# Second expert layer, mixing of a token's two expert outputs: the first scaling on ScalarE, the scaled addition on VectorE

## The chip, the cores and the metric

One core of a Trainium2 chip runs the kernel. The metric is the device time in microseconds, the median over runs. A profiled execution gives the rows below; it is one execution, and its own time is given beside its span.

The engines are named as in the profile: PE is TensorE's matmul, PEld its weight load, DVE is VectorE, ACT is ScalarE, POOL is GpSimd and SP is SyncE.

## What is computed

The model has four blocks, each an attention and an expert layer, on 2 x 1024 tokens of width 256. The change lies in the expert layer of the second block. For each token it takes the two experts with the largest gate, mixes their outputs with the gates as weights and multiplies the mixture by one more matrix:

```python
gating = jax.nn.softmax(X @ Wg + bg, axis=-1)
top_k_indices = jnp.argsort(gating, axis=-1)[..., -TOPK:]      # TOPK = 2, 8 experts
h1 = jnp.einsum('bsd,edh->bseh', X, W1) + b1
h3 = jnp.einsum('bsd,edh->bseh', X, W3) + b3
h = jax.nn.silu(h1 * h3)
expert_outputs = jnp.einsum('bseh,eho->bseo', h, W2) + b2
topk_out = jnp.take_along_axis(expert_outputs, top_k_indices[..., None], axis=2)
topk_w = jnp.take_along_axis(gating, top_k_indices, axis=-1)
mixed = jnp.sum(topk_w[..., None] * topk_out, axis=2)
return mixed @ Wf + bf
...
x = x + jnp.tanh(g_ffn[1]) * _L1_ffn_ref(_layernorm(x, axis=-1), ...)
```

The last four lines of the function, from `topk_out` on, and the addition to `x` are the part that the change is about.

## The kernel before

The layer is `l1_ffn`. It keeps 2048 tokens as 16 tiles of 128 (`TILES`), 256 columns each. Every engine has a program of its own, written out in order, and engines wait for each other on semaphores; no scheduler moves anything. Between two layers all engines meet at a barrier, so the next layer (an attention) starts when the last engine has ended this one.

Most of the layer is a loop over experts and their tiles of routed tokens. It ends with each token's two expert outputs in the memory `outs`. Then comes the mixing, which is all that the change touches:

- SyncE loads the first outputs, ScalarE the second ones, in four quarters of four tiles each (`load_outputs`, L896), into `fetched[:, k, t, :]`. The quarter's two loads count up `fetched_part[q]`. All eight loads are issued at once, after `all_stored`.
- VectorE makes the mixture of tile t in `mixed[:, t % 4, :]`, a ring of four buffers. L1157 multiplies the first output by its weight (a tensor_scalar with a pointer operand), L1158 multiplies the second by its own and adds L1157's result (a scalar_tensor_tensor). Both go through `Steps`: it counts `mix_steps` up when the instruction is complete and makes VectorE itself wait for that count before it goes on. Behind the mixture of tile t VectorE adds tile t - 2 to `x` (`add_output`, L1148).
- TensorE transposes the mixture in two pieces (`turn_mixed`, L1017) into one of two banks of `p_h`. It then multiplies by `wf` (L1029, two matmuls of 256 columns, each of which stands as two rows in the profile) into one of two other banks. Its order is: transposition of tile t + 1, then product of tile t. The product of tile t waits for `added`, the addition of tile t - 2.
- ScalarE copies the transposed mixture from the bank to `mixed_t` (L1066), a ring of four.

In the prediction "transposition of tile t", "copy of tile t", "product of tile t" and "addition of tile t" are these steps.

## Time and profile before

| | us |
|---|---|
| median of three runs | 3202.24 |
| lowest and highest | 3200.54, 3202.68 |
| profiled execution, its own time | 3204.76 |
| its span | 3203.0 |
| TensorE busy | 2851.1 (89%) |
| VectorE busy | 1890.4 (59%) |
| ScalarE busy | 1432.0 (45%) |
| GpSimd busy | 586.9 (18%) |
| TensorE's granted clock, mean | 0.931 |

The busy times are averages over some ten layers with different limits. The mixing runs from the first landing at 1010.76 us to the end of the last addition at 1035.78 us. What happens in it is read from the windows, the waits and the timeline of that stretch. The timeline joins rows of one kind; "x4" is four rows, and "x8" at the end are the products of two tiles. The bracket at the end of a row is the idle time of the engine before it, and what ended it. A row of the windows gives the stretch, its length, then the busy time (and the count of instructions) of PE, PEld, DVE, ACT and POOL, the granted clock, the busy share of the DMA engines and what they moved. The granted clock is given as a share: 1.00 is 2.4 GHz and 0.50 is 1.2 GHz.

### The profile page before, as it was taken

How to read it: one execution, taken by the hardware profiler on the slowest of the kernel's cores; microseconds unless marked ns; L12 is line 12 of the kernel's file. 1: busy time of each engine (PE TensorE's matmuls, PEld its weight loads, DVE VectorE, ACT ScalarE, POOL GpSimd, SP SyncE). 2: the span in 40 equal slices, each digit the busy share in tenths (PEclk: the TensorE clock that was granted, in tenths of full speed). 3: DMA queues.
4: the chain of work that ended last, by engine and by line, in shares of the span. 5: the costliest groups of instructions: out<-in, count | busy, mean ns of one | idle time of the engine just before them, and what ended most of it. 6: DMA issues, size and time to landing. Idle time of an engine off the chain costs nothing. (4 is left out here: it accounts for less than half of the span.)

```text
span 3203.0 us, 46363 instructions
## 1 busy us (share of the span) xinstructions
PE 2851.1 (89%) x13988; PEld 2126.9 (66%) x13989; DVE 1890.4 (59%) x3602; ACT 1432.0 (45%) x2987; POOL 586.9 (18%) x655
## 2 busy tenths in 40 slices
PE   5796779986997989999689999999999999968996
PEld 4795545546886779999456666666666666646665
DVE  4414465516555354443588888878788888664443
ACT  1233544431211224544347766767676777711111
POOL 0133010001442200000200000000000000106776
PEclk8698879996999779999799999999999999979999
DMA  1342022223232010000112323233222332335776
GB/s 40 107 163 92 1 32 23 22 11 117 84 103 81 13 40 27 26 13 1 24 25 24 31 22 31 22 33 31 31 21 30 23 31 22 13 72 149 162 173 144
DMA packets 153723, 168.84 MB, mean 53 GB/s; under 512 B 38128, under 2 KB 123014, under 8 KB 153286
## 3 DMA queue, kind: packets, MB, share of 16 engines
q1 hardware_dynamic: 115878, 105.16, 20.2%
q0 software_dynamic: 21280, 37.93, 5.5%
q10 hardware_dynamic: 16416, 24.12, 2.3%
q8 instruction: 50, 0.82, 0.1%
q14 instruction: 99, 0.81, 0.1%
HBM read 105.77 MB, written 29.84 MB: 42 GB/s over the span
## 5 line engine op out<-in xcount | busy, mean ns | idle before, releaser
L2036 ACT ACTIVATE l3a_pt_hi<-l3a_banks 128x512 fp32r<-128x512 f32 (+2 forms) x640 | 382.9, 598 | 326.6 <-PE l3a_banks L1977 272.4
L2147 DVE TENSOR_TENSOR l3a_pt_lo<-l3a_pt,l3a_pt_hi 128x512 fp32r<-128x512 f32 (+2 forms) x640 | 459.9, 727 | 75.9 <-ACT l3a_pt L2037 38.8
L2037 ACT ACTIVATE l3a_pt<-l3a_banks 128x512 f32<-128x512 f32 (+2 forms) x640 | 378.7, 592 | 0.0
L2117 DVE TENSOR_REDUCE l3a_maxima<-l3a_banks 128x1 f32<-128x1178 f32 x256 | 351.5, 1375 | 3.5 <-PE l3a_banks L1924 3.3
L2182 POOL TENSOR_TENSOR l3a_out_t<-l3a_out,l3a_shared 64x512 f32<-64x512 f32 x65 | 90.3, 1390 | 1134.2 <-DMA l3a_shared<-l3a_inverse 1134.2
L1977 PE MATMUL l3a_banks<-l3a_pt_hi,l3a_v 128*65 128x512 f32 (+2 forms) x640 | 287.7, 449 | 6.1 <-ACT l3a_out L2051 3.8
L1990 PE MATMUL l3a_banks<-l3a_q,l3a_k 128*128 128x512 f32 (+2 forms) x640 | 253.9, 397 | 13.0 <-ACT l3a_pt L2037 11.4
L1991 PE MATMUL l3a_banks<-l3a_q,l3a_k 72*128 72x512 f32 (+5 forms) x640 | 252.8, 395 | 0.0
L1977 PE MATMUL l3a_banks<-l3a_pt_lo,l3a_v 128*65 128x512 f32 (+2 forms) x640 | 251.9, 394 | 0.0
L1977 PE MATMUL l3a_banks<-l3a_pt_hi,l3a_v_lo 128*65 128x512 f32 (+2 forms) x640 | 251.8, 393 | 0.0
L1924 PE MATMUL l3a_banks<-l3a_k,l3a_q 128*128 128x512 f32 (+1 forms) x768 | 207.3, 378 | 16.0 <-DVE l3a_maxima L2117 16.0
L1924 PEld LDWEIGHTS l3a_banks<-l3a_k,l3a_q 128*128 128x128 f32 x768 | 137.8, 190 | 63.8 <-DVE l3a_maxima L2117 40.2
L1990 PEld LDWEIGHTS l3a_banks<-l3a_q,l3a_k 128*128 128x128 f32 (+2 forms) x640 | 115.2, 180 | 78.5 <-ACT l3a_pt L2037 16.4
L1610 ACT ACTIVATE l2f_hidden_hi<-l2f_p_h,l2f_b_pair 128x512 fp32r<-128x512 f32 x128 | 89.5, 699 | 150.0 <-PE l2f_p_h L1563 139.9
L2934 POOL DMA_INDIRECT l3f_sums<-l3f_y_rows,l3f_token_index x96 | 147.7, 1539 | 41.3 <-issue 24.1
L1977 PE MATMUL l1a_banks<-l1a_pt,l1a_v 128*65 128x512 f32 (+2 forms) x320 | 151.6, 596 | 1.7 <-ACT l1a_out L2051 1.7
L1662 DVE TENSOR_TENSOR l2f_hidden_lo<-l2f_hidden,l2f_hidden_hi 128x512 fp32r<-128x512 f32 x128 | 88.6, 692 | 107.8 <-ACT l2f_hidden L1611 107.8
L1002 PE MATMUL l1f_p_h<-l1f_xt_tile,l1f_w 128*128 128x128 f32 x1184 | 141.6, 279 | 7.1 <-issue 6.2
L1002 PEld LDWEIGHTS l1f_p_h<-l1f_xt_tile,l1f_w 128*128 128x128 f32 x1184 | 137.2, 194 | 14.6 <-issue 14.4
L3030 PE MATMUL l3f_p_h<-l3f_xt,l3f_w 128*128 128x320 f32 x512 | 144.8, 436 | 1.2 <-DVE l3f_xt L3192 1.2
L1577 PE MATMUL l2f_p_y<-l2f_w_hi,l2f_hidden_lo 128*128 128x256 f32 x512 | 144.7, 283 | 0.0
L1577 PE MATMUL l2f_p_y<-l2f_w_hi,l2f_hidden_hi 128*128 128x256 f32 x512 | 144.6, 282 | 0.0
(583 smaller groups left out, 5876.7 us busy)
## 6 DMA issues: line engine op xcount, KB each, us to landing
l3f_w<-in_L_ffn_w SPq DMA_DIRECT2D x96, 256.0 KB, 3.7
l0f_w<-in_L_ffn_W ACTq DMA_DIRECT2D x12, 1024.0 KB, 6.5
l1f_w<-in_L_ffn_W ACTq DMA_DIRECT2D x18, 512.0 KB, 4.6
l3a_shared<-l3a_inverse SPq DMA_DIRECT2D x65, 128.0 KB, 6.3
l2f_w<-in_L_ffn_w SPq DMA_DIRECT2D x16, 512.0 KB, 4.5
l3a_q<-l3a_q SPq DMA_DIRECT2D x64, 128.0 KB, 2.3
l3a_k<-l3a_k SPq DMA_DIRECT2D x64, 128.0 KB, 2.3
l0f_w<-in_L_ffn_W SPq DMA_DIRECT2D x4, 1024.0 KB, 7.2
```

Source lines behind the costliest of these rows:

```text
L1002: ins = pe.matmul(p_h[:, bank, (f % 2) * P:(f % 2 + 1) * P], w[:, u, c, f * P:(f + 1) * P], xt_tile[:, c * P:(c + 1) * P], start=c == 0, s ...
L1577: ins = pe.matmul(p_y[:, bank, half * D:(half + 1) * D], h[:, n % 2, f, j * P:(j + 1) * P], a[:, u, 1, f * D:(f + 1) * D], start=f == 0 an ...
L1924: ins = pe.matmul(banks[:, c, 0:end - at], lhs, a.k1[:, u, h, at:end], start=True, stop=not masked)
L1977: ins = pe.matmul(a.o_bank[0:HEAD + 1, :], v[0:rows, u, c, h, :], pt[0:rows, slot, :], start=c == 0 and k == 0, stop=c == KEY_CHUNKS - 1 a ...
L1990: pe.matmul(a.st_bank[0:rows, n % 2, :], a.k1[:, u, h, row:row + rows], a.q1[:, u, h, queries], start=True, stop=False)
L1991: pe.matmul(a.st_bank[0:rows, n % 2, :], a.k2[second, u, h, row:row + rows], a.q2[second, u, h, queries], start=False, stop=True).then_inc ...
L2036: act.activation(a.pt_hi[0:rows, n % a.pt_slots, :], a.st_bank[0:rows, n % 2, :], ACT.Exp, bias=bias, scale=scale)
L2037: act.activation(a.pt[0:rows, n % 4, :], a.st_bank[0:rows, n % 2, :], ACT.Exp, bias=bias, scale=scale).then_inc(a.exped, 1)
L2117: dve.tensor_reduce(a.maxima[:, n:n + 1], banks.rearrange("p a b -> p (a b)")[:, 0:KEYS], AX.X, ALU.max).then_inc(a.maxed, 1)
L2147: dve.tensor_tensor(a.pt_lo[0:rows, slot, :], a.pt[0:rows, n % 4, :], a.pt_hi[0:rows, slot, :].bitcast(F32), ALU.subtract).then_inc(a.lo_m ...
L2934: pool.indirect_dma_start(sums, bass.IndirectOffsetOnAxis(token_index[0:n, u, j:j + 1], 0), y_rows[0:n, u, j, :], None, compute_op=ALU.add ...
L3030: ins = pe.matmul(p_h[:, k + f, 0:CAP], w[:, u, c, f * P:(f + 1) * P], xt[:, c, u * CAP:(u + 1) * CAP], start=c == 0, stop=c == DC - 1)
```

## The change

The first multiplication of every tile moves from VectorE to ScalarE. ScalarE multiplies tiles 0 and 1 ahead of its loop, and in turn t of the loop tile t + 2, ahead of the copy of tile t. For that it now waits for the quarters of `fetched` and, from tile 4 on, for the transposition four tiles back, which frees the buffer. A new semaphore `first_scaled` tells VectorE. VectorE waits for it and keeps the scaled addition, without waiting for its own result; `mix_steps` counts one a tile and not two, and TensorE waits for t + 1.

```diff
--- before.py
+++ after.py
@@ -881,6 +881,7 @@
             "routed", "exped", "chose", "ranked", "route_steps", "lanes_shown", "inverted", "placed", "x_loaded",
             "x_turned", "x_kept", "h_done", "h3_kept", "h13_kept", "h_kept", "y_done", "y_kept", "y_stored",
             "all_stored", "y_free", "passed", "mix_steps", "mixed_turned", "mixed_kept", "out_done", "added", "biased"))
+        first_scaled = sem("first_scaled")
         w_loaded = [sem("w_loaded0"), sem("w_loaded1")]
         indexed, out_indexed, first_loaded, x_ready, taken, summed, out_placed = sem("indexed"), sem("out_indexed"), sem("first_loaded"), sem("x_ready"), sem("taken"), sem("summed"), sem("out_placed")
         fetched_part = [sem(f"fetched{q}") for q in range(4)]
@@ -1010,7 +1011,7 @@
                         ins.then_inc(y_done, 1)
 
             def turn_mixed(t):
-                pe.wait_ge(mix_steps, 2 * t + 2)
+                pe.wait_ge(mix_steps, t + 1)
                 if t >= 2:
                     pe.wait_ge(mixed_kept, t - 1)
                 for c in range(DC):
@@ -1059,7 +1060,18 @@
             act.wait_ge(all_stored, 1)
             for q in range(4):
                 load_outputs(act, 1, q)
+            def scale_first(t):
+                if t % 4 == 0:
+                    act.wait_ge(fetched_part[t // 4], K * 16)
+                if t >= 4:
+                    act.wait_ge(mixed_turned, t - 3)
+                act.mul(mixed[:, t % 4, :], fetched[:, 0, t, :], weight[:, 0, t:t + 1]).then_inc(first_scaled, 1)
+
+            scale_first(0)
+            scale_first(1)
             for t in range(TILES):
+                if t + 2 < TILES:
+                    scale_first(t + 2)
                 act.wait_ge(mixed_turned, t + 1)
                 if t >= 4:
                     act.wait_ge(out_done, t - 3)
@@ -1151,12 +1163,9 @@
             for t in range(TILES):
                 if t % 4 == 0:
                     dve.wait_ge(fetched_part[t // 4], K * 16)
-                if t >= 4:
-                    dve.wait_ge(mixed_turned, t - 3)
-                mix = Steps(dve, mix_steps, 2 * t)
-                mix(dve.tensor_scalar(mixed[:, t % 4, :], fetched[:, 0, t, :], weight[:, 0, t:t + 1], None, ALU.mult))
-                mix(dve.scalar_tensor_tensor(mixed[:, t % 4, :], fetched[:, 1, t, :], weight[:, 1, t:t + 1], mixed[:, t % 4, :],
-                                             ALU.mult, ALU.add))
+                dve.wait_ge(first_scaled, t + 1)
+                dve.scalar_tensor_tensor(mixed[:, t % 4, :], fetched[:, 1, t, :], weight[:, 1, t:t + 1], mixed[:, t % 4, :],
+                                         ALU.mult, ALU.add).then_inc(mix_steps, 1)
                 if t >= 2:
                     add_output(t - 2)
             for t in range(TILES - 2, TILES):
```

How the instructions stand on VectorE, from the third tile of the mixing on, before. `l1f_mixed` is the mixture, `l1f_fetched` the two outputs, `chip_x` is x and `l1f_p_h` the banks:

```order
L1157 TENSOR_SCALAR l1f_mixed<-l1f_fetched,l1f_weight 128x256
L1158 SCALAR_TENSOR_TENSOR l1f_mixed<-l1f_fetched,l1f_weight,l1f_mixed 128x256
L1148 SCALAR_TENSOR_TENSOR chip_x<-l1f_p_h,chip_gates,chip_x 128x256
L1157 TENSOR_SCALAR l1f_mixed<-l1f_fetched,l1f_weight 128x256
L1158 SCALAR_TENSOR_TENSOR l1f_mixed<-l1f_fetched,l1f_weight,l1f_mixed 128x256
L1148 SCALAR_TENSOR_TENSOR chip_x<-l1f_p_h,chip_gates,chip_x 128x256
L1157 TENSOR_SCALAR l1f_mixed<-l1f_fetched,l1f_weight 128x256
L1158 SCALAR_TENSOR_TENSOR l1f_mixed<-l1f_fetched,l1f_weight,l1f_mixed 128x256
L1148 SCALAR_TENSOR_TENSOR chip_x<-l1f_p_h,chip_gates,chip_x 128x256
```

And with the change, from the first tile on:

```order
L1167 SCALAR_TENSOR_TENSOR l1f_mixed<-l1f_fetched,l1f_weight,l1f_mixed 128x256 x3
L1160 SCALAR_TENSOR_TENSOR chip_x<-l1f_p_h,chip_gates,chip_x 128x256
L1167 SCALAR_TENSOR_TENSOR l1f_mixed<-l1f_fetched,l1f_weight,l1f_mixed 128x256
L1160 SCALAR_TENSOR_TENSOR chip_x<-l1f_p_h,chip_gates,chip_x 128x256
L1167 SCALAR_TENSOR_TENSOR l1f_mixed<-l1f_fetched,l1f_weight,l1f_mixed 128x256
L1160 SCALAR_TENSOR_TENSOR chip_x<-l1f_p_h,chip_gates,chip_x 128x256
L1167 SCALAR_TENSOR_TENSOR l1f_mixed<-l1f_fetched,l1f_weight,l1f_mixed 128x256
```

The row of L1157 has gone; one scaled addition and one addition to x alternate, behind three scaled additions at the start.

On ScalarE before, from the loads on; `l1f_mixed_t` is the transposed mixture:

```order
L896 DMA l1f_fetched<-l1f_outs 128x4x256 x4
L1066 COPY l1f_mixed_t<-l1f_p_h 128x256 x16
L843 UNCONDITIONAL_BRANCH
```

With the change, the same place:

```order
L897 DMA l1f_fetched<-l1f_outs 128x4x256 x4
L1068 ACTIVATE l1f_mixed<-l1f_fetched,l1f_weight 128x256 x3
L1078 COPY l1f_mixed_t<-l1f_p_h 128x256
L1068 ACTIVATE l1f_mixed<-l1f_fetched,l1f_weight 128x256
L1078 COPY l1f_mixed_t<-l1f_p_h 128x256
L1068 ACTIVATE l1f_mixed<-l1f_fetched,l1f_weight 128x256
L1078 COPY l1f_mixed_t<-l1f_p_h 128x256
L1068 ACTIVATE l1f_mixed<-l1f_fetched,l1f_weight 128x256
```

Three scalings stand ahead of the first copy, then one ahead of each further copy. The loads keep their place ahead of all of them. TensorE's and SyncE's instructions keep their order.

## Rows read from the trace of the kernel before

**Rows 1.** The page, engines: busy us, share of the span, instructions.

```profile
PE 2851.1 (89%) x13988; PEld 2126.9 (66%) x13989; DVE 1890.4 (59%) x3602; ACT 1432.0 (45%) x2987; POOL 586.9 (18%) x655
```

**Rows 2.** Windows of the mixing: us, busy us of each engine, clock, DMA share, GB/s.

```profile
1013.00:1016.00 3.00, 3.00 (x10) 2.42 (x9) 1.32 (x4) 0.75 (x2) 0.00 (x0) 0.50 1.09 348
1016.00:1019.00 3.00, 2.66 (x14) 1.97 (x13) 2.45 (x7) 0.75 (x2) 0.00 (x0) 0.98 1.00 317
...
1025.00:1028.00 3.00, 2.88 (x15) 1.97 (x16) 2.72 (x7) 0.75 (x2) 0.00 (x0) 1.00 0.00 0
```

**Rows 3.** Waits from 1016 to 1036 us: us in total, times, longest.

```profile
PEld l1f_p_h L1017 <- DVE l1f_mixed L1158: 5.8, 12, 0.7
DVE chip_x L1148 <- PE l1f_p_h L1029: 2.5, 9, 0.8
```

**Rows 4.** Timeline: start us, us, engine, line, what. The last tiles.

```profile
1030.63 1.03 PE L1029 MATMUL l1f_p_h<-l1f_wf,l1f_mixed_t 128*128 128x256 f32 x4
...
1031.77 0.48 DVE L1148 SCALAR_TENSOR_TENSOR chip_x<-l1f_p_h,chip_gates,chip_x 128x256 f32<-128x256 f32 x1
...
1032.17 0.34 DVE L1157 TENSOR_SCALAR l1f_mixed<-l1f_fetched,l1f_weight 128x256 f32<-128x256 f32 x1
...
1032.55 0.48 DVE L1158 SCALAR_TENSOR_TENSOR l1f_mixed<-l1f_fetched,l1f_weight,l1f_mixed 128x256 f32<-128x256 f32 x1
...
1033.09 0.44 PE L1017 MATMUL l1f_p_h<-chip_ident,l1f_mixed 128*128 128x128 f32 x2
...
1033.36 1.89 PE L1029 MATMUL l1f_p_h<-l1f_wf,l1f_mixed_t 128*128 128x256 f32 x8
...
1034.43 0.48 DVE L1148 SCALAR_TENSOR_TENSOR chip_x<-l1f_p_h,chip_gates,chip_x 128x256 f32<-128x256 f32 x1 [0.76 <-PE l1f_p_h L1029]
1035.30 0.48 DVE L1148 SCALAR_TENSOR_TENSOR chip_x<-l1f_p_h,chip_gates,chip_x 128x256 f32<-128x256 f32 x1 [0.38 <-PE l1f_p_h L1029]
```

**Rows 5.** Timeline, where the clock has just risen.

```profile
1016.76 1.03 PE L1029 MATMUL l1f_p_h<-l1f_wf,l1f_mixed_t 128*128 128x256 f32 x4
...
1017.60 0.48 DVE L1158 SCALAR_TENSOR_TENSOR l1f_mixed<-l1f_fetched,l1f_weight,l1f_mixed 128x256 f32<-128x256 f32 x1
1018.12 0.48 DVE L1148 SCALAR_TENSOR_TENSOR chip_x<-l1f_p_h,chip_gates,chip_x 128x256 f32<-128x256 f32 x1
```

**Rows 6.** Timeline, TensorE at the lower clock.

```profile
1013.08 1.91 PE L1029 MATMUL l1f_p_h<-l1f_wf,l1f_mixed_t 128*128 128x256 f32 x4
...
1014.79 0.63 PE L1017 MATMUL l1f_p_h<-chip_ident,l1f_mixed 128*128 128x128 f32 x2
...
1015.21 1.49 PE L1029 MATMUL l1f_p_h<-l1f_wf,l1f_mixed_t 128*128 128x256 f32 x4
```

**Rows 7.** ScalarE groups of 128x256, by shape: busy us, mean ns, idle before.

```profile
L1047 ACT ACTIVATE l1f_hidden<-l1f_h 128x256 f32<-128x256 f32 x37 | 15.5, 418 | 116.9 <-DVE l1f_h L1138 116.9
...
L2450 ACT ACTIVATE chip_xt<-l1p_pt,l1p_columns 128x256 f32<-128x256 f32 x16 | 7.8, 487 | 5.0 <-PE l1p_pt L2405 5.0
...
L1066 ACT COPY l1f_mixed_t<-l1f_p_h 128x256 f32<-128x256 f32 x16 | 6.0, 373 | 28.1 <-PE l1f_p_h L1017 28.1
```

**Rows 8.** Timeline, the first tile.

```profile
1010.76 0.35 DVE L1157 TENSOR_SCALAR l1f_mixed<-l1f_fetched,l1f_weight 128x256 f32<-128x256 f32 x1 [9.44 <-DMA l1f_fetched<-l1f_outs]
1011.15 0.49 DVE L1158 SCALAR_TENSOR_TENSOR l1f_mixed<-l1f_fetched,l1f_weight,l1f_mixed 128x256 f32<-128x256 f32 x1
...
1011.78 0.66 PE L1017 MATMUL l1f_p_h<-chip_ident,l1f_mixed 128*128 128x128 f32 x2 [11.03 <-DVE l1f_mixed L1158]
```

**Rows 9.** Timeline of ScalarE, the copy of tile 2.

```profile
1015.46 0.37 ACT L1066 COPY l1f_mixed_t<-l1f_p_h 128x256 f32<-128x256 f32 x1 [1.76 <-PE l1f_p_h L1017]
```

**Rows 10.** Transfers: ScalarE's second and last load, KB, us from issue to landing.

```profile
l1f_fetched<-l1f_outs ACTq DMA_DIRECT2D x1, 512.0 KB, 9.3
...
l1f_fetched<-l1f_outs ACTq DMA_DIRECT2D x1, 512.0 KB, 13.7
```

**Rows 11.** The loads by line: duration ns min/median/max, first and last start us.

```profile
L896 ACTq DMA_DIRECT2D l1f_fetched<-l1f_outs x4: 471/531/1463, 1004.7 to 1006.3; - x4
```

## The prediction

> **What bounds the kernel now.** I read the page first: TensorE is busy 89% of the span [rows 1], so an instruction taken off VectorE is worth something only where TensorE waits for it. The change touches only the last part of the second expert layer, the mixing: sixteen token tiles between 1010.8 and 1035.8 us of a span of 3203.0, under 1% of it. The table of windows over that stretch comes next [rows 2]. It falls in two. Until about 1016 us TensorE runs at the lower granted clock (0.50, 1.2 GHz), VectorE is idle for more than half of the window and the transfers fill the DMA engines. From then on the clock is 1.00 (2.4 GHz), and in the window from 1025 to 1028 TensorE is busy 2.88 of 3.00 us and VectorE 2.72. Busy shares do not say which of them holds the other, so the third view is that of the waits from 1016 us on [rows 3]: the weight load of a transposition waits 12 times for the scaled addition (L1158), and VectorE's addition to x (L1148) waits 9 times for TensorE. Two engines that wait for each other in turn are a ring, and the timeline shows it [rows 4].
>
> I number the tiles by counting back from the end: the row of eight matmuls at 1033.36 is the output product of tiles 14 and 15, and the last L1157 and L1158 (1032.17, 1032.55) are tile 15. Then one turn of the ring reads as follows. The product of tile 12 starts at 1030.63. Its sum lets VectorE add tile 12 to x at 1031.77, after 1.14. VectorE takes up L1157 of tile 15 at 1032.17, after 0.40. L1158, which waits for L1157's result, starts at 1032.55, after 0.38. The transposition of tile 15 starts at 1033.09, after 0.54, and the product of tile 14 at 1033.36, after 0.27. 1.14 + 0.40 + 0.38 + 0.54 + 0.27 = 2.73 us for two tiles, and the start-to-start distance of products 12 and 14 is 2.73 as well. So the whole period is this chain: nothing in it is slack, and a term taken out of it shortens the stage. Two such rings, of even and odd tiles, run interleaved.
>
> **What the change removes.** L1157 goes from VectorE, sixteen times 0.345. In the ring it stands as 0.38 between the addition to x and L1158. Without it a round is 2.73 - 0.38 = 2.35. What is late next is TensorE's own work. Two products with nothing between them release their additions 0.87 apart (1034.43 and 1035.30), and a pair of transpositions takes 0.27, the start of tile 15's to that of the product behind it [rows 4]. That is 1.14 a tile, 1.15 rounded up, and 2.30 for two, only 0.05 under the new ring. Nearly all of the 0.38 should be had, and no more than 0.43 can be.
>
> Where does it count? The first product at the full clock is tile 2's, at 1016.76; the last pair starts at 1033.36 [rows 4, 5]. These are 16.60 us for six rounds. Six at 2.73 are 16.38; the other 0.22 is in the first, where VectorE reached the addition of tile 2 late, behind L1158. New: 6 x 2.35 = 14.10, a saving of 16.60 - 14.10 = 2.50. At TensorE's own pace it would be 12 x 1.15 = 13.80, a saving of 2.80. Ahead of 1016.76 I count no gain: there the product of tile 0 starts at 1013.08 and TensorE is at half its clock; the product and the transpositions follow without a wait for VectorE [rows 6]. Behind the last product nothing changes.
>
> The self-wait behind L1158 goes too. It delays the next instruction of VectorE (0.52 from L1158 to the addition of tile 2 against 0.40 from that kind of addition to L1157) [rows 4, 5]. In the steady part the addition waits for TensorE anyway; I count it only inside the 0.22 above.
>
> **What it adds.** ScalarE gets sixteen scalings of 128x256. The trace has none from SBUF with a pointer scale. Nearest rows [rows 7]: L1047, 128x256 from SBUF, 0.418; L2450, 128x256 with two pointer operands, 0.487; below them the copy L1066, 0.37. I take 0.42, since L1047 reads the same memory and shape. ScalarE then works 0.42 + 0.37 = 0.79 a tile, with the upper end 0.86, against a period of 1.17. The copy of a tile comes behind the scaling two tiles ahead, and that scaling can start as soon as the copy before it has ended. So 0.37 + 0.49 must fit between two copies 1.17 apart, which leaves 0.3. Cost on the path: none; the cover is ScalarE's idle time, and it would be gone if a scaling took over 0.8.
>
> Only the first tile has nobody ahead of it. Now L1157 starts at 1010.76 and L1158 at 1011.15, 0.39 later [rows 8]. After: the scaling 0.42 and a hop from engine to engine of 0.54 - 0.48 = 0.06, so L1158's successor starts 0.48 after the landing: 0.09 later. With the rows at the ends, 0.37 and 0.487, it is 0.04 to 0.16. All that follows moves by that.
>
> The Trainium skill ("ScalarE: Activation LUTs", What ACT_TABLE_LOAD costs) gives 186 ns, 0.833 ns an element and some 93 ns for a pointer operand, by which this scaling would be an estimated 0.49 us and the start 0.16 later. The same page (Rules for kernel authors) says to multiply on VectorE and not on ScalarE, which speaks against the change. Per instruction the trace agrees (0.345 on VectorE, nothing on ScalarE under 0.37), but the rule weighs the instruction and not who is being waited for.
>
> **The new waits.** The second to fourth quarter of the rows are now waited for on ScalarE also, two tiles early, with a copy queued behind. The scaling of tile 4 stands ahead of the copy of tile 2, which starts at 1015.46 now [rows 9]. The second quarter's loads are issued some 0.5 behind the first's at 1004.7, and the later one lands after 9.3, at about 1014.5 [rows 10, 11]. The scaling ends by 1015.0 and the copy starts as before. The last quarter lands at about 1006.3 + 13.7 = 1020.0, and the scaling of tile 12, ahead of the copy of tile 10, comes some five microseconds after that. The ring of four buffers asks for the transposition four tiles back, long done. No DMA is moved.
>
> **Sum.** -2.50 + 0.09 = -2.41. Between the bounds: -2.80 + 0.04 = -2.76, and -2.50 + 0.16 = -2.34. Against the profiled execution: 3204.76 - 2.4 = 3202.4. That one is 2.5 above the median of the three runs, 3202.24; against the median 3199.8, which is my forecast.
>
> **Rivals.**
>
> *TensorE's pace, or a better start.* The new period is 1.15 a tile and the start costs nothing: 3202.24 - 2.8 = 3199.4. For it: the two bounds are 0.05 a round apart. Against it: every round in the rows is a sum of latencies.
>
> *No gain; the change does not do what it says.* The scaling comes too late from ScalarE, or the addition on VectorE finds another wait of the same size: 0 in the rounds, +0.09 at the start, 3202.3. For it: the waits on TensorE in [rows 3] would be there with any late input. Against it: the scaling has a full tile in hand.
>
> *ScalarE stands before a landing (slower).* If the second quarter lands with the last, at 1020.0, the copy of tile 2 ends at 1020.0 + 0.42 + 0.37 = 1020.8 and its product starts at 1020.9 and not 1016.76: +4.1, so 3202.24 - 2.4 + 4.1 = 3203.9. It decides from a landing at 1015.9 on (0.9 ahead of 1016.76), and eats the whole gain at 1018.3. The rows have the quarters land one behind the other, with 1.4 to spare.
>
> *The clock (slower).* In the trace it rises at about 1016, after TensorE has worked since 1011.78 [rows 2, 8]. Were it to stay at 0.50, a product would take 1.71 and two transpositions 0.42 (starts at 1013.08, 1014.79 and 1015.21 [rows 6]), 2.13 a tile and not 1.17: 0.96 more for each of some 11 tiles, 3199.8 + 10.6 = 3210.4. It eats the gain if the rise comes 2.4 / 0.45 = 5.3 us later (0.96 lost in 2.13 is 0.45 per us). For it: the stage starts 0.09 later and all later stages start 2.4 earlier. Against it: TensorE is as busy as before in the slices ahead of the rise. The opposite is as possible in a later stage: an earlier rise, a few microseconds saved.
>
> The Trainium skill ("TensorE: Matmul & The Clock Gate", Part 1) says that the clock is throttled by default, released by activity, and that the moment varies from run to run with the phase of the kernel. By that the rise could move in both directions here; the trace of one run cannot show it.
>
> **Chances.** Forecast 0.70; TensorE's pace 0.08; no gain 0.09; ScalarE at a landing 0.04; a clock later here or further on 0.05, earlier 0.04. The measurement can tell about 0.2%, 6.4 us, from no change, and only the clock cases reach that: faster 0.04, same 0.92, slower 0.04. The range takes in 3199.4 and 3202.3, and around them what the three runs show (1.7 below their median, 0.4 above) and as much again below and above for a clock edge that moves in another stage: 3196.8 to 3203.6. What is left out are the large clock moves and the late landing.
>
> **What would show it.** In the profile after: the products of tiles 12 and 14 start 2.35 apart, not 2.73; the stage, from the first landing to the last addition, is 2.4 shorter; the scalings on ScalarE take 0.37 to 0.49; the copies keep waiting for TensorE and not for a landing; TensorE's wait for L1158's successor falls from 5.8 to under 1 and its place is taken by its own work. I am wrong if the period stays at 2.73 (another chain ran beside this one), if copies start behind a scaling that waits for a landing, or if the clock's rise moves by more than a microsecond.

## The result, and the profile after

| | median us | runs | profiled run | its span |
|---|---|---|---|---|
| before | 3202.40 | 3200.54 to 3202.68 (4) | 3204.76 | 3203.0 |
| after | 3182.05 | 3180.52 to 3187.06 (4) | 3187.06 | 3185.3 |

The changed kernel takes 0.994 of the time of the kernel before, with an interval of 0.9923 to 0.9958. A later pair of series gave 0.9937 (0.9924 to 0.9951). The kernel before has a fourth run here (3202.57), which moves its median from 3202.24 to 3202.40. The forecast was a gain of 2.4 us. The gain is 20.4 us, and the time lies 14.8 us below the range.

**The mixing.** The first step is to ask whether the change did what it was forecast to do. The timeline after, two tiles of the steady part, columns as in [rows 4]; L1160 is the addition to x (L1148 before), L1167 the scaled addition (L1158), L1068 the new scaling on ScalarE, L1078 the copy (L1066):

```profile
1027.23 0.48 DVE L1160 SCALAR_TENSOR_TENSOR chip_x<-l1f_p_h,chip_gates,chip_x 128x256 f32<-128x256 f32 x1 [0.31 <-PE l1f_p_h L1030]
1027.25 1.03 PE L1030 MATMUL l1f_p_h<-l1f_wf,l1f_mixed_t 128*128 128x256 f32 x4
...
1028.32 0.48 DVE L1160 SCALAR_TENSOR_TENSOR chip_x<-l1f_p_h,chip_gates,chip_x 128x256 f32<-128x256 f32 x1 [0.21 <-PE l1f_p_h L1030]
...
1028.72 0.48 DVE L1167 SCALAR_TENSOR_TENSOR l1f_mixed<-l1f_fetched,l1f_weight,l1f_mixed 128x256 f32<-128x256 f32 x1
1028.90 0.51 ACT L1068 ACTIVATE l1f_mixed<-l1f_fetched,l1f_weight 128x256 f32<-128x256 f32 x1
...
1029.30 0.39 PE L1018 MATMUL l1f_p_h<-chip_ident,l1f_mixed 128*128 128x128 f32 x2
...
1029.53 1.03 PE L1030 MATMUL l1f_p_h<-l1f_wf,l1f_mixed_t 128*128 128x256 f32 x4
```

The ring of [rows 4] reads here: product at 1027.25, addition to x 1.07 later, scaled addition 0.40 later, transposition 0.58 later, product 0.23 later. The sum is 2.28 for two tiles, where it was 2.73. L1157's 0.38 is gone and the product's addition comes 0.07 sooner. From the first landing to the end of the last addition the mixing took 25.02 before (1010.76 to 1035.78) and takes 22.34 now (1011.87 to 1034.21). That is 2.68 less, where the forecast had 2.41. The waits from 1017 to 1034 us and the window that answers to the last of [rows 2]:

```profile
ACT l1f_mixed_t L1078 <- PE l1f_p_h L1018: 6.1, 14, 0.8
DVE chip_x L1160 <- PE l1f_p_h L1030: 5.0, 15, 0.9
PEld l1f_p_h L1018 <- DVE l1f_mixed L1167: 2.8, 12, 0.3
```

```profile
1024.00:1027.00 3.00, 3.00 (x17) 2.19 (x16) 2.40 (x6) 2.20 (x6) 0.00 (x0) 1.00 0.00 0
```

TensorE is busy for the whole window (2.88 of 3.00 in [rows 2]), and VectorE now waits for it.

**The other 18 us** cannot be in these 25. I measured every stage of both traces on TensorE, from its first instruction on the tiles of the stage to its last. The last attention (L2616 and the functions it calls; tiles `l3a_`), which the change does not touch, went from 1251.5 to 1230.8, 20.8 less. No other stage moved by more than 3.3; the span as a whole is 17.7 shorter. The main part of the last attention is a loop (L2260 before, in `attention_units`) of six turns, and the difference comes in five steps of about 4, one at each of its five branches back. The waits there, 1570 to 2820 before and 1570 to 2800 after (columns as in [rows 3]; L2147 and L2156 are one line, as are L1990 and L1999). Before:

```profile
DVE l3a_pt_lo L2147 <- ACT l3a_pt L2037: 38.8, 94, 1.0
...
DVE l3a_pt_lo L2147 <- issue: 30.4, 5, 6.1
...
PEld l3a_banks L1990 <- ACT l3a_pt L2037: 16.4, 10, 2.0
```

After:

```profile
DVE l3a_pt_lo L2156 <- ACT l3a_pt L2046: 48.9, 99, 2.3
...
PEld l3a_banks L1999 <- ACT l3a_pt L2046: 7.1, 5, 1.6
```

Before, VectorE stood still five times for 6.1 us, once a turn, with "issue" as the reason: it waited for nothing that the profile shows. After, there is no such wait. The timeline of VectorE before, the first instruction behind each of three branches back (the first, second and fifth):

```profile
1853.88 0.69 DVE L2147 TENSOR_TENSOR l3a_pt_lo<-l3a_pt,l3a_pt_hi 128x512 fp32r<-128x512 f32 x1 [6.13 <-issue]
...
2004.04 0.69 DVE L2147 TENSOR_TENSOR l3a_pt_lo<-l3a_pt,l3a_pt_hi 128x512 fp32r<-128x512 f32 x1 [6.09 <-issue]
...
2454.68 0.69 DVE L2147 TENSOR_TENSOR l3a_pt_lo<-l3a_pt,l3a_pt_hi 128x512 fp32r<-128x512 f32 x1 [6.06 <-issue]
```

Four turns take 600.80, one 150.20. The same after, at two successive branches:

```profile
1851.39 0.69 DVE L2156 TENSOR_TENSOR l3a_pt_lo<-l3a_pt,l3a_pt_hi 128x512 fp32r<-128x512 f32 x1 [2.07 <-ACT l3a_pt L2046]
...
1997.56 0.69 DVE L2156 TENSOR_TENSOR l3a_pt_lo<-l3a_pt,l3a_pt_hi 128x512 fp32r<-128x512 f32 x1 [2.28 <-ACT l3a_pt L2046]
```

A turn takes 146.17, 4.03 less; five times that is 20.2, nearly all of the 20.8. One more row differs: the queue that loads instructions. Over four turns (1856 to 2456 before, 1850 to 2450 after; packets, MB, share), first before, then after:

```profile
q14 instruction: 44, 0.36, 0.2%
```

```profile
q14 instruction: 21, 0.17, 0.1%
```

Eleven packets a turn became five. On the page of the profile the queue has 99 packets before and 70 after. So the engines load less code while they loop, and the stop of VectorE goes with those loads: within its stop at the second branch (1997.95 to 2004.04) packets start at 2001.9 and 2002.1, and one at 2004.0, as it ends.

What can an edit in another layer do to this loop? It changes where its code stands. Counted in the two compiled programs, the change takes 30 instructions from VectorE ahead of the loop (multiplications, self-waits and waits for a buffer) and adds 19 to ScalarE. The body of the loop is 342 instructions long on VectorE and 400 on ScalarE. In the table below "V" is the place of VectorE's body and "S" that of ScalarE's: the number of its first instruction in its engine's program, modulo 256, and that plus the length. What a runtime may put ahead is not counted, so the places are good up to a constant.

### The profile page after: what moved, and what is told of

It reads as the page before. It is cut to its first block and busy times, and to the rows that moved or that the text cites. A ratio compares the mean times of both kernels' runs of the same rounds, so it can differ in the third digit from the quotient of the medians.

```text
span 3185.3 us, 46352 instructions
## 1 busy us (share of the span) xinstructions
PE 2844.1 (89%) x13988; PEld 2130.7 (67%) x13989; DVE 1885.8 (59%) x3586; ACT 1436.7 (45%) x3003; POOL 586.2 (18%) x655
## 5 line engine op out<-in xcount | busy, mean ns | idle before, releaser
L2156 DVE TENSOR_TENSOR l3a_pt_lo<-l3a_pt,l3a_pt_hi 128x512 fp32r<-128x512 f32 (+2 forms) x640 | 460.0, 727 | 55.8 <-ACT l3a_pt L2046 48.9
L1999 PE MATMUL l3a_banks<-l3a_q,l3a_k 128*128 128x512 f32 (+2 forms) x640 | 253.5, 396 | 6.1 <-ACT l3a_pt L2046 4.6
L1999 PEld LDWEIGHTS l3a_banks<-l3a_q,l3a_k 128*128 128x128 f32 (+2 forms) x640 | 115.2, 180 | 69.6 <-ACT l3a_pt L2046 7.1
```

What stands on the lines that cost most here:

```text
L1999: pe.matmul(a.st_bank[0:rows, n % 2, :], a.k1[:, u, h, row:row + rows], a.q1[:, u, h, queries], start=True, stop=False)
L2156: dve.tensor_tensor(a.pt_lo[0:rows, slot, :], a.pt[0:rows, n % 4, :], a.pt_hi[0:rows, slot, :].bitcast(F32), ALU.subtract).then_inc(a.lo_m ...
```

## Experiments

My theory: the time goes with the place of the two loop bodies. The rival: it goes with the mixing (its end, the phase of the clock) or with what ScalarE and VectorE now do in it. Where the edit is filler, the filler is increments of a semaphore that nobody waits for afterwards. Each ratio is to the runs of before taken beside the kernel: 3201.39 for c1 to c4, 3203.52 for d1 to d3, 3204.63 for e1 to e4. The mixing, the last attention and q14 (the packets of the instruction queue on the page) are from one trace each. d3, e3 and e4 have a single run: they are read from their traces, and their times carry no verdict.

| kernel | time, us (runs) | ratio, interval | mixing | last attention | V | S | q14 |
|---|---|---|---|---|---|---|---|
| before | 3202.40 (4) | | 25.02 | 1251.5 | 147 to 489 | 57 to 457 | 99 |
| after | 3182.05 (4) | 0.9923 to 0.9958 | 22.34 | 1230.8 | 117 to 459 | 76 to 476 | 70 |
| c1_dve30 | 3201.99 (10) | 0.9989 to 1.0012 | 22.65 | 1250.3 | 147 to 489 | 76 to 476 | 95 |
| c2_act19 | 3202.25 (10) | 0.9989 to 1.0010 | 25.20 | 1250.1 | 147 to 489 | 76 to 476 | 94 |
| c3_dve227 | 3208.19 (10) | 1.0011 to 1.0031 | 24.74 | 1241.5 | 118 to 460 | 57 to 457 | 76 |
| c4_noself | 3188.44 (4) | 0.9933 to 0.9966 | 24.75 | 1241.3 | 133 to 475 | 57 to 457 | 74 |
| d1_noself_act19 | 3176.13 (4) | 0.9900 to 0.9933 | 24.81 | 1229.9 | 133 to 475 | 76 to 476 | 69 |
| d2_act140 | 3179.48 (4) | 0.9912 to 0.9953 | 22.82 | 1231.3 | 117 to 459 | 216 to 616 | 70 |
| d3_double | 3184.43 (1) | | 22.72 | 1229.6 | 117 to 459 | 92 to 492 | 69 |
| e1_after_again | 3182.43 (5) | 0.9924 to 0.9951 | 22.00 | 1231.6 | 117 to 459 | 76 to 476 | 69 |
| e2_noself_act19_again | 3180.93 (5) | 0.9916 to 0.9943 | 24.44 | 1230.1 | 133 to 475 | 76 to 476 | 69 |
| e3_noself_act10 | 3178.10 (1) | | 24.67 | 1229.1 | 133 to 475 | 67 to 467 | 69 |
| e4_noself_act256 | 3197.09 (1) | | 24.89 | 1247.3 | 133 to 475 | 57 to 457 | 76 |

**c1: the change, with VectorE's code moved back to its old place.**

```diff
@@ after, l1f, VectorE @@
             dve.wait_ge(biased, 4)
+            for _ in range(30):
+                dve.sem_inc(h3_kept, 1)
```

> The changed kernel with 30 semaphore increments added to VectorE's program behind its expert loop, while it waits for the first landing. VectorE's later code stands again where it stands in the kernel before (the change takes 30 instructions from it). Everything else is the change. Theory C (where VectorE's loop body in the last attention lies among the code blocks that are fetched decides whether VectorE stalls at each branch back): the last attention is 20 us longer again, VectorE has five idle times of about 6 us before L2156 that nothing released, the queue of instruction fetches has some 99 packets, and the time is 3182 + 20 = 3200 (3198 to 3202). Theory A (it is ScalarE's code, 19 instructions longer): stays at 3182. Theory M (the mixing itself, or the phase in which the later layers start): stays at 3182. In all three the mixing stays at 22.3 us from the first landing to the end of the last addition.

3201.99: all of the gain is gone, with the mixing still at 22.65. Its waits in the last attention and two rows of its timeline, the first and fifth branch:

```profile
DVE l3a_pt_lo L2158 <- issue: 30.5, 5, 6.1
```

```profile
1851.19 0.69 DVE L2158 TENSOR_TENSOR l3a_pt_lo<-l3a_pt,l3a_pt_hi 128x512 fp32r<-128x512 f32 x1 [6.13 <-issue]
...
2450.31 0.69 DVE L2158 TENSOR_TENSOR l3a_pt_lo<-l3a_pt,l3a_pt_hi 128x512 fp32r<-128x512 f32 x1 [6.08 <-issue]
```

The five stops are back and a turn takes 149.78, with ten packets. The 30 instructions stand in the mixing's own layer, 800 us ahead, and do nothing. That the shorter mixing brings the 20 us is ruled out.

**c2: the kernel before, with ScalarE's code where the change puts it.** The same filler, 19 `act.sem_inc(h_kept, 1)` behind the loads of ScalarE.

> The kernel before with 19 semaphore increments added to ScalarE's program behind its loads in the second expert layer, as many instructions as the change adds to it. The mixing is as before. Theory C: 3202, the five idle times of VectorE stay. Theory A: 3182 to 3185. Theory M: 3202.

3202.25, no difference. ScalarE's place alone brings 1.4 of the last attention and nothing that the time shows while VectorE stops. ScalarE's own gap at the branch, 3.3 to 3.6 in the kernel before, has fallen under 2, and a turn takes ten packets and not eleven.

**c3: the kernel before, with VectorE's code moved on by 227,** which modulo 256 is 29 back. The filler stands where c1's does, 227 times.

> The kernel before with 227 semaphore increments added to VectorE's program behind its expert loop: its later code is moved on so that it stands in its block of 256 instructions as it does with the change. The mixing is as before. Theory C: the last attention is 20 us shorter, so 3202 - 20 = 3182, plus what the increments themselves cost beyond the 9.4 us in which VectorE waits there (0 to 5 us): 3182 to 3188. Theories A and M: 3202 or up to 5 more.

The last attention is 10.0 shorter and VectorE's stops are gone, though instructions were added: what counts is the place, not the number. The expected 3182 to 3188 was missed. The time as a whole is worse, since the increments took about 0.09 us each on VectorE, some 20 us, of which 11.2 lengthened the expert layer; the attention behind it is 6.2 longer. And only half of the 20.8 came. The other half stood on ScalarE, which has five gaps of 3.4 to 3.5 us at the branches. The next kernel shows them without filler.

**c4: the kernel before, without the self-wait of L1158.** A second way to move VectorE's code, by 14 instructions back, without filler.

```diff
@@ before, VectorE @@
-                mix(dve.scalar_tensor_tensor(mixed[:, t % 4, :], fetched[:, 1, t, :], weight[:, 1, t:t + 1], mixed[:, t % 4, :],
-                                             ALU.mult, ALU.add))
+                dve.scalar_tensor_tensor(mixed[:, t % 4, :], fetched[:, 1, t, :], weight[:, 1, t:t + 1], mixed[:, t % 4, :],
+                                         ALU.mult, ALU.add).then_inc(mix_steps, 1)
```

> The kernel before, but VectorE doesn't wait for its own scaled addition L1158; both multiplications stay on VectorE. Ring of latencies (the forecast's): the period of two tiles stays at 2.73, since the addition waits for TensorE, and only the first round gets 0.2 shorter: the mixing takes 24.8 us and not 25.0. Rival (VectorE's own work sets the period): 0.13 less a tile, 2.47 for two, mixing 23.0. For the last attention: 14 instructions fewer on VectorE, between the kernel before (stalls) and the change (30 fewer, none). Theory C gives the one or the other, 3202 or 3182, and nothing between; it tells where the block's edge is. Theory A: 3202.

3188.44, with the mixing at 24.75: the scaling is still on VectorE and the gain is 13 us. That lies between the two values of theory C, which allowed nothing between. In the mixing the period did not stay at 2.73 but is 2.66. VectorE has no stop of its own left. Its waits in the last attention:

```profile
ACT l3a_pt_hi L2036 <- PE l3a_banks L1977: 272.8, 299, 4.1
DVE l3a_pt_lo L2147 <- ACT l3a_pt L2037: 63.9, 106, 3.4
...
PEld l3a_banks L1990 <- ACT l3a_pt L2037: 17.0, 10, 2.5
```

And the timeline at the first branch back:

```profile
1842.43 0.59 ACT L2037 ACTIVATE l3a_pt<-l3a_banks 128x512 f32<-128x512 f32 x1
...
1847.14 0.60 ACT L2036 ACTIVATE l3a_pt_hi<-l3a_banks 128x512 fp32r<-128x512 f32 x1 [4.12 <-PE l3a_banks L1977]
...
1848.26 0.69 DVE L2147 TENSOR_TENSOR l3a_pt_lo<-l3a_pt,l3a_pt_hi 128x512 fp32r<-128x512 f32 x1 [3.39 <-ACT l3a_pt L2037]
1848.28 0.19 PEld L1990 LDWEIGHTS l3a_banks<-l3a_q,l3a_k 128*128 128x128 f32 x1 [2.54 <-ACT l3a_pt L2037]
```

ScalarE stops for 4.12 us and VectorE and TensorE wait for it. The row names TensorE as the releaser, but the record of ScalarE's own register instruction (L2027), which stands ahead of L2036 and waits for nobody, starts only at 1847.0 and has 3.96 idle ahead of it. So the engine itself was stopped, as VectorE was. In the kernel before, this stop lay beside the 6.1 of VectorE, and taking it away alone (c2) brought next to nothing. The instruction queue from 1844 to 2444, a little over four turns; a single turn has six packets:

```profile
q14 instruction: 26, 0.21, 0.1%
```

**d1: c4 and c2 together.** Both bodies at favourable places, the scalings not moved.

> The kernel before without VectorE's wait for its own L1158 (14 instructions fewer on VectorE) and with 19 semaphore increments added to ScalarE's program behind its loads: both multiplications stay on VectorE, but the code of both engines in the last attention stands where it doesn't stall. Theory C in its second form (both places count, each worth some 10 us: with VectorE's stalls gone the last attention still took 1241 and ScalarE stalled 3.3 us at each branch back; with both gone it took 1231): last attention 1231, mixing 24.8, time 3188 - 10 = 3178 to 3181, which is the change's time without its mixing. Rival (ScalarE's place alone does nothing, and the change's last 10 us come from its mixing): stays at 3188.

3176.13, the fastest series and below the expected 3178 to 3181, with the mixing at its old 24.81. The same kernel takes 3180.93 in e2, on another chip; the two ratios overlap. The last attention is as short as after the change. Its waits there and its timeline at the first, second and fifth branch:

```profile
ACT l3a_pt_hi L2038 <- PE l3a_banks L1979: 262.4, 300, 2.5
DVE l3a_pt_lo L2149 <- ACT l3a_pt L2039: 49.4, 102, 2.1
```

```profile
1842.04 0.69 DVE L2149 TENSOR_TENSOR l3a_pt_lo<-l3a_pt,l3a_pt_hi 128x512 fp32r<-128x512 f32 x1 [2.09 <-ACT l3a_pt L2039]
...
1987.93 0.69 DVE L2149 TENSOR_TENSOR l3a_pt_lo<-l3a_pt,l3a_pt_hi 128x512 fp32r<-128x512 f32 x1 [2.02 <-ACT l3a_pt L2039]
...
2425.71 0.69 DVE L2149 TENSOR_TENSOR l3a_pt_lo<-l3a_pt,l3a_pt_hi 128x512 fp32r<-128x512 f32 x1 [2.04 <-ACT l3a_pt L2039]
```

A turn takes 145.92. 19 instructions on ScalarE that do nothing are worth 11.4 us of the last attention here, and nothing in c2: two stops beside each other, of which the longer one sets the time.

**d2: the change, with ScalarE's code moved on by 140** (a new semaphore `filler`, incremented 140 times at the head of the last attention).

> The changed kernel with 140 semaphore increments on ScalarE at the start of the last attention, while it waits for TensorE's first transposition there. ScalarE's loop body of 400 instructions then starts near the start of a block of 256 and lies in two blocks. Theory C (a body that lies in two blocks is never fetched again; one that lies in three is fetched again at each branch back, five packets a time): the queue of instruction fetches falls from 70 packets to about 45, TensorE's waits for ScalarE at the branch (L1999, 5 times, 1.1 to 1.6 us) go, the last attention gets 5 to 8 us shorter (1223 to 1226) and the time is 3174 to 3177. Rival (these fetches are hidden by now): fetches fall, time stays at 3182. If the increments aren't hidden they cost up to 10 us ahead of the loop.

The last attention is 1231.3: no stop came back, nor did the loads fall under five packets a turn. The filler itself is one row of the waits, and lies beside a load of the bias that TensorE waits for anyway:

```profile
ACT l3a_ln L2739 <- issue: 8.9, 1, 8.9
```

The expectation rested on a rule for ScalarE (a body in two blocks of 256 instructions is not loaded again, one in three is), and that rule failed here.

**d3: the change, with every scaling done twice,** once more into a scratch tile, which leaves the result as it is.

```diff
@@ after, ScalarE @@
+                act.mul(scratch[:, t, :], fetched[:, 0, t, :], weight[:, 0, t:t + 1])
                 act.mul(mixed[:, t % 4, :], fetched[:, 0, t, :], weight[:, 0, t:t + 1]).then_inc(first_scaled, 1)
```

> The changed kernel with a second scaling of each tile on ScalarE into a buffer that nobody reads. It tests the cover in which the scaling is hidden. ScalarE's work a tile is then 0.51 + 0.51 + 0.37, with the starts 0.45 apart some 1.3 us, over the period of 1.14. Ring of latencies with ScalarE's idle time as cover: the period goes from 1.14 to 1.25 to 1.4 a tile and ScalarE is the bound, the mixing takes 24 to 26 us. Rival (ScalarE isn't near the path at all): the period stays at 1.14. The last attention stays at 1231 (ScalarE's place moves by 16 instructions within the same half of a block).

The mixing took 22.72 and its period stayed at 2.27 for two tiles. The expected 1.25 to 1.4 a tile did not come; the rival, that ScalarE is nowhere near the path, held. Groups of lines, 1010 to 1035 us (instructions x count, busy, mean ns, idle before):

```profile
L1069 ACT ACTIVATE l1f_scratch<-l1f_fetched,l1f_weight 128x256 f32<-128x256 f32 x16 | 8.1, 508 | 10.9 <-DMA l1f_fetched<-l1f_outs 10.9
L1070 ACT ACTIVATE l1f_mixed<-l1f_fetched,l1f_weight 128x256 f32<-128x256 f32 x16 | 7.9, 496 | 0.0
```

ScalarE has 0.51 + 0.50 + 0.37 = 1.38 a tile by their durations, over the period of 1.14, and still keeps up, because neighbouring instructions overlap by some 0.1. Its timeline:

```profile
1017.30 0.37 ACT L1080 COPY l1f_mixed_t<-l1f_p_h 128x256 f32<-128x256 f32 x1 [0.72 <-PE l1f_p_h L1019]
1017.57 0.51 ACT L1069 ACTIVATE l1f_scratch<-l1f_fetched,l1f_weight 128x256 f32<-128x256 f32 x1
1017.98 0.50 ACT L1070 ACTIVATE l1f_mixed<-l1f_fetched,l1f_weight 128x256 f32<-128x256 f32 x1
```

From start to start these are 0.27 and 0.41; with another 0.41 behind the second scaling, an estimate from the first, a tile takes ScalarE 1.09, just under the period. The cover of one scaling was larger than the forecast had it.

**e1 and e2: the change and d1 once more, beside each other on the same chip.**

> The changed kernel itself, once more, beside the next one on the same chip. Both have both loop bodies of the last attention at the favourable places; this one has the mixing moved as well, the next one has not. If the change's own edit is worth the 2.4 to 2.7 us that the mixing shows, this one is that much faster than the next; if the mixing's gain is given back further on (a clock edge, the first router), the two are equal within 2 us. From the two runs so far on different chips (3182.05 against 3202.4 of before; 3176.13 against 3203.52 of before) I lean to equal or slower by a few us.

> The kernel before without the self-wait of L1158 and with 19 increments on ScalarE, once more: no scaling moved. Mixing 24.8 us long, last attention 1230, no stall at the branch on VectorE or ScalarE. By the theory of the mixing 2.5 us slower than the changed kernel beside it; by what was measured so far a few us faster.

3182.43 (3180.54 to 3185.86) with the mixing moved and 3180.93 (3175.97 to 3181.77) without. In the two traces the mixing is 22.00 and 24.44, so the 2.4 us are there; the times do not show them. The stage behind, the third layer's first attention (`l2a_`), took 120.4 in e1 and 114.0 in e2. Windows from there, columns as in [rows 2], first e1, then e2:

```profile
1040.00:1050.00 10.00, 8.12 (x23) 4.71 (x24) 4.67 (x13) 0.59 (x1) 1.36 (x1) 0.50 0.00 0
1050.00:1060.00 10.00, 9.32 (x35) 7.22 (x34) 3.77 (x11) 4.15 (x11) 0.00 (x0) 0.50 0.00 1
1060.00:1070.00 10.00, 10.00 (x34) 8.06 (x33) 1.78 (x5) 2.02 (x6) 2.62 (x3) 0.50 0.01 2
```

```profile
1040.00:1050.00 10.00, 6.17 (x24) 3.18 (x24) 6.29 (x22) 0.58 (x1) 1.36 (x1) 0.67 0.00 1
1050.00:1060.00 10.00, 8.87 (x41) 7.59 (x40) 3.80 (x11) 4.74 (x12) 0.00 (x0) 0.67 0.00 0
1060.00:1070.00 10.00, 10.00 (x40) 8.00 (x38) 2.07 (x6) 1.43 (x5) 2.62 (x3) 0.65 0.01 2
```

In e1 the granted clock stays at 0.50 for 30 us, in e2 it is at 1.00 for a third of them. Over all twelve profiles without c3, this stage took 115.8 to 120.4, mean 119.0, in the five kernels with the moved mixing and 112.5 to 118.5, mean 116.1, in the seven without. The 2.9 between the means are as large as the gain of the mixing. Its spread is that of the clock: it spends between 32.3 and 53.1 us at 0.50, and the stage less half of that time is 94.7 to 97.2 in all thirteen profiles. That the moved mixing causes the longer time at 0.50 is not shown: it is one profile for each kernel, and the two groups overlap.

**e3: c4 with 10 increments on ScalarE; e4: c4 with 256,** at the head of the last attention as in d2.

> As the kernel before without the self-wait (3188.4, last attention 1241.3, ScalarE stalls 5 times 3.2 to 4.0 us at the branch back), with 10 increments on ScalarE and not 19. It looks for the place at which ScalarE's stall goes. If the stall shrinks in proportion (a refetch that runs ahead of the branch by some instructions), ScalarE's idle time at the branch is about 2 us and the last attention about 1236; if there is an edge between 0 and 10, it is gone and the stage is 1230; if the edge is between 10 and 19, the stage stays at 1241.

> The kernel before without the self-wait, with 256 increments on ScalarE at the head of the last attention, so that its loop body stands at the same place within 256 instructions as without any. If the place counts modulo 256 instructions, ScalarE's stall is there as in the kernel without increments: 5 times 3.2 to 4.0 us, the last attention about 1241 plus what the increments take at its head (140 of them took 8.9 us of ScalarE and 0.5 of the stage). If it is the sheer number that counts, or something that shifts with it such as the time of the branch, there is no stall and the stage is about 1231.

With 10 the last attention is 1229.1 and there is no stop: the edge lies between 0 and 10 instructions, and the gain does not come in proportion. With 256 the stop is back, at each of the five branches, where 10 and 19 had taken it away. ScalarE in e4, first and fifth:

```profile
1856.24 0.60 ACT L2036 ACTIVATE l3a_pt_hi<-l3a_banks 128x512 fp32r<-128x512 f32 x1 [3.51 <-PE l3a_banks L1977]
...
2448.55 0.60 ACT L2036 ACTIVATE l3a_pt_hi<-l3a_banks 128x512 fp32r<-128x512 f32 x1 [3.24 <-PE l3a_banks L1977]
```

A turn takes 148.08 and six packets, as in c4, and not the five of e3. So for ScalarE too it is the place that counts and not the number, and the place comes round after 256 instructions. Whether it comes round after 128 already, neither this run nor c3 can tell (see "What stays open"). The stage is at 1247.3 and not at 1241.3 since the increments at its head take their own time: ScalarE spends 16.7 us on them, and the turns behind are no longer than in c4.

## Why the prediction was wrong, point by point

**The step that failed** is "Behind the last product nothing changes." It looked at data and at the clock only. Five branches back stood behind it, each with a stop of 6.1 us on VectorE that is there or not by how many instructions stand ahead. The profile of the kernel before held the evidence: a wait of 30.4 us in five parts with "issue" as the reason, at the top of a loop, and 99 packets on the instruction queue. What it did not hold is where the edge is: c4 shows that 14 instructions fewer are enough on VectorE, e3 that 10 more are enough on ScalarE. So the forecast could have named the case, with a gain of up to 20 us and a loss if a later loop is moved onto an edge, and not its sign. The rivals had no such case, and that is why the range was too narrow by 14.8 us.

**How the 20.4 divide.** By pairs that differ in one place: VectorE's, 10.2 us of the last attention (before to c4), then ScalarE's 11.4 (c4 to d1). In the other order it is 1.4 for ScalarE (before to c2) and 20.2 for VectorE (c2 to d1), so the shares belong to the order and only the sum of 21.6 to both. With VectorE put back, c1, nothing of the gain is left in the time. The mixing's own gain, 2.68 in the trace, is not visible in the time where the places are alike: c1 against c2, 3201.99 and 3202.25, and e1 against e2. A gain of 2.4 could not be told there: the interval of c1 against before (0.9989 to 1.0012) reaches from 3.5 us less to 3.8 more.

**The mechanism in the mixing was right.** The ring was the chain and L1157 a link of it. Of its terms:

- The ring was put at 2.35 and measured 2.28. A round gained 0.45, more than the 0.38 of the forecast and than the 0.43 that it put as the most. The other 0.07 is VectorE's wait for its own L1158. The forecast left it out of the steady part because the addition "waits for TensorE anyway", which misreads [rows 4]: the addition of tile 12 at 1031.77 has no bracket, so VectorE did not stand idle for TensorE. It comes 0.53 behind the L1158 of tile 14 (the row below), so the 1.14 from product to addition held 0.07 of that wait; after, it is 1.07. c4 takes the self-wait away alone, and its products start 2.66 apart, not 2.73. Of the other terms one grew by 0.04 (0.54 to 0.58) and one fell by as much (0.27 to 0.23). TensorE's pace, the rival with 0.08, described the steady part better than the forecast: TensorE is busy all the time. The row, from the trace before:

```profile
1031.24 0.48 DVE L1158 SCALAR_TENSOR_TENSOR l1f_mixed<-l1f_fetched,l1f_weight,l1f_mixed 128x256 f32<-128x256 f32 x1
```

- TensorE's wait for the scaled addition was to fall from 5.8 to under 1. It fell to 2.8, at most 0.3 at a time, all of it on the weight load.
- The scaling was taken as 0.42, with a range to 0.487, and took 0.51, 16 times. The Trainium skill ("ScalarE: Activation LUTs", What ACT_TABLE_LOAD costs) had given 0.49 by an estimate; that and the row of L2450 (0.487) were the nearest prices.
- The start: L1167 begins at 1012.52, 0.65 behind the landing, not 0.48, which is 0.26 later than before and not 0.09. At the first product 0.08 of it is left: 2.40 behind the landing, 2.32 before. The rows:

```profile
1011.87 1.31 ACT L1068 ACTIVATE l1f_mixed<-l1f_fetched,l1f_weight 128x256 f32<-128x256 f32 x3 [10.95 <-DMA l1f_fetched<-l1f_outs]
1012.52 1.28 DVE L1167 SCALAR_TENSOR_TENSOR l1f_mixed<-l1f_fetched,l1f_weight,l1f_mixed 128x256 f32<-128x256 f32 x3 [10.10 <-ACT l1f_mixed L1068]
...
1014.27 2.08 PE L1030 MATMUL l1f_p_h<-l1f_wf,l1f_mixed_t 128*128 128x256 f32 x4
...
1016.04 0.51 ACT L1068 ACTIVATE l1f_mixed<-l1f_fetched,l1f_weight 128x256 f32<-128x256 f32 x1 [1.15 <-DMA l1f_fetched<-l1f_outs]
...
1016.81 0.37 ACT L1078 COPY l1f_mixed_t<-l1f_p_h 128x256 f32<-128x256 f32 x1 [0.26 <-PE l1f_p_h L1018]
```

- ScalarE did stand ahead of a landing, 1.15 us for the second quarter, as the slower rival had it. The copy behind it then waited another 0.26 for TensorE, so nothing was lost. The forecast had the quarter land in time and the scaling done by 1015.0; it started at 1016.04, with 0.26 to spare.
- The clock rose (granted clock from 0.50 to 1.00) at 1017.6, 5.7 behind the first landing, and at 1016.1, 5.3 behind, before: 0.4 apart, under the microsecond allowed.
- The range's ends do not follow from the rows. From 3199.4 and 3202.3 the spread of the runs gives 3197.7 and 3202.7; the 0.9 beyond, each way, was an allowance for a clock edge that no row measures.

**What stays open.** Why the edge is where it is. The Trainium skill ("Runtime: NRT & Kernel Launch", Instruction fetch mechanics) says that most engines hold two blocks of 256 instructions and that a branch to a target outside them has to load before it can go on. That a stop comes at a branch, with loads on the instruction queue, agrees (before, c1, c4), and so does e4, where 256 more instructions bring the stop back. That VectorE's body of 342 fits two blocks at 133 to 475 and not at 147 to 489 agrees only if some 24 to 37 instructions stand ahead that I don't count. ScalarE does not agree, whatever stands ahead: a body of 400 fits two blocks from 113 neighbouring places, and the places without a stop (67, 76, 92 and 216) lie in no such stretch that leaves out 57, since from 67 to 216 it is 150.

Blocks of 128 fit the record better. This is worked out from the traces afterwards, and no run tests it.

- The fillers of 227 and 256 cannot tell the two apart: 227 is 29 back by both counts. By 128, the 216 of d2 is 88, between the 76 and 92 that do not stop either.
- One packet goes with some 128 instructions: e4 has 256 more than c4 and 76 packets against 74. The five packets a turn that remain look like ScalarE's. After the change, three of them start at 1889.5, 1937.1 and 1983.8, that is 47.6 and 46.7 apart, and 128 of 400 instructions in a turn of 146.17 us take 46.8. In d2, which is 12 instructions further on by this count, the third of the five comes 31.8 behind the second, and not 36.5.
- With 24 to 37 uncounted instructions on VectorE and 61 to 70 on ScalarE, ScalarE's body touches five blocks of 128 at 57 and four at its other places, and VectorE's touches four at 147 and three at its others. The packets of a turn are then one more than the blocks for a body that touches four or five, and none for one that touches three: 6 + 5 = 11 in the kernel before, 5 + 5 = 10 in c1 and c2, 6 in c3, c4 and e4, and 5 in the rest. All thirteen traces have these numbers.

It leaves open why VectorE stops for 6.1 us with four blocks, while ScalarE with four has no gap over 2, as it has elsewhere in the turn. A test would be c4 with 128 empty instructions more on ScalarE: if the period is 128, the stop of 3.2 to 4.1 is there, and if there is none, it is not 128. Whether the clock in the attention behind eats the mixing's gain is open also.

## What to carry to other kernels

When an edit adds or removes instructions on an engine, look at every loop that stands behind it on that engine, in other stages too: an idle time with "issue" as its reason at the top of each turn, and a count of the instruction queue that grows with the turns, say that the loop's place matters, and the edit moves it. Such a difference must be put down to the place and not to the edit, by putting as many empty instructions back as were removed; here that took the whole gain away. And a loop like this can be tuned by itself: 14 instructions fewer on VectorE and 10 to 19 empty ones on ScalarE brought as much as the change (e2 against e1), with the scalings left where they were.

## What the runs showed of the hardware

- A branch back stopped VectorE for 6.1 us (body of 342 instructions) or not at all, and ScalarE for 3.2 to 4.1 (body of 400) or not by so much; an offset of 14 and of 10 instructions decided it. With 256 more the stop was back (e4); a period of 128 would do the same and fits all thirteen traces, but was not tested.
- The instruction queue's packets are of some 8 KB (0.81 MB in 99), and 256 more instructions brought two more packets (e4 against c4). A turn of the loop took eleven in the kernel before, ten with VectorE's stops alone (c1, c2), six with ScalarE's alone (c3, c4, e4), five with none.
- Two engines that stop at the same branch hide each other: freeing VectorE brought 10.2 of the last attention, freeing ScalarE then 11.4, and freeing ScalarE first 1.4.
- An increment of a semaphore took about 0.09 us on VectorE (227 in some 20 us) and 0.064 on ScalarE (8.9 / 140).
- The clock explains the spread of the attention behind: 112.5 to 122.2 us in the thirteen traces, with 32.3 to 53.1 at 0.50.
- A releaser named in a row is a guess: ScalarE's stop in c4 is put down to a matmul, while a register instruction ahead of it had not been issued.
- A scaling of 128x256 from SBUF by a pointer took 0.51 us on ScalarE, and 0.41 from start to start when another stood behind it.
